# Last feed-forward product with standing weights and 512 moving tokens, in a four-block kernel

## What is computed

```python
h = silu(_tlin(x, w1_w, w1_s)) * _tlin(x, w2_w, w2_s)     # 128 -> 512
h = gelu(_tlin(h, h1_w, h1_s))                            # 512 -> 512, exact gelu
h = gelu(_tlin(h, h2_w, h2_s))                            # 512 -> 512
return _tlin(h, w3_w, w3_s)                               # 512 -> 128, added to x
```

## Time and profile before

| what | value |
|---|---|
| median of 3 runs | 1786.47 us (1783.78 to 1786.57) |
| profiled execution, its own time | 1786.55 us |
| its span, first to last instruction | 1781.5 us |
| stage two, from 1387 us to the end | some 394 us |
| one sequence in the steady part of stage two | 22.67 us |
| busy of the span: PE, DVE, ACT, POOL | 84%, 85%, 72%, 62% |

### The profile page before, as it was taken

The page is one execution under the profiler, slowest core; times in us unless marked ns, Lnnn a source line. Parts: engine busy times, 40 slices in busy tenths (PEclk is TensorE's granted clock), DMA queues, the critical chain, the costliest instruction groups (busy, mean ns, idle before and its releaser), DMA issues. The chain is left out here.

```text
span 1781.5 us, 24641 instructions
## 1 busy us (share of the span) xinstructions
PE 1502.4 (84%) x8039; PEld 807.3 (45%) x8039; DVE 1519.0 (85%) x2837; ACT 1284.4 (72%) x2176; POOL 1103.6 (62%) x987
## 2 busy tenths in 40 slices
PE   4245788888889888888888888888898799999997
PEld 1122343333334333333433334333434588888886
DVE  6899999999999999999999999997331688988883
ACT  5665888988989898898989889895555454444441
POOL 5884776868577686867768586775122255555552
PEclk9996999999999999999999999999999699999998
DMA  4000000000000000000000000000200000000000
GB/s 136 0 1 0 18 13 7 19 1 19 1 19 16 4 19 1 18 1 19 17 3 19 1 19 1 18 15 5 84 3 17 1 7 12 13 13 13 13 13 19
DMA packets 14543, 27.41 MB, mean 15 GB/s; under 512 B 3837, under 2 KB 4550, under 8 KB 13898
## 3 DMA queue, kind: packets, MB, share of 16 engines
q1 hardware_dynamic: 14410, 25.79, 5.2%
HBM read 9.00 MB, written 4.19 MB: 7 GB/s over the span
## 5 line engine op out<-in xcount | busy, mean ns | idle before, releaser
L616 POOL TENSOR_TENSOR sum_fast<-sum_fast,state_fast 128x512 f32<-128x512 f32 x448 | 573.9, 1281 | 78.1 <-DVE state_fast L598 38.0
L598 DVE TENSOR_TENSOR_SCAN state_fast<-state_fast,bank 128x512 f32<-128x512 f32 x512 | 602.7, 1202 | 0.7 <-ACT bank L567 0.7
L1008 ACT ACTIVATE prob_fast<-bank 128x1024 f32<-128x1024 f32 x320 | 326.0, 1020 | 122.1 <-PE bank L992 111.7
L992 PE MATMUL bank<-stacks_fast 64*128 64x512 f32 (+3 forms) x2048 | 361.4, 462 | 50.0 <-ACT prob_fast L1008 46.6
L583 ACT ACTIVATE state_fast<-chan_all_kept,neg_a_fast 128x512 f32<-128x512 f32 x512 | 340.1, 713 | 10.6 <-POOL sum_fast L616 8.5
L1052 POOL TENSOR_SCALAR_AFFINE_SELECT prob_fast<-prob_fast 128x512 f32<-128x512 f32 x256 | 159.9, 636 | 293.6 <-ACT prob_fast L1008 292.1
L992 PEld LDWEIGHTS bank<-stacks_fast 64*128 64x128 f32 x2048 | 170.7, 185 | 250.0 <-ACT prob_fast L1008 150.8
L1069 PE MATMUL bank<-prob_fast,v_ext_fast 128*32 128x512 f32 (+3 forms) x2048 | 177.7, 442 | 8.1 <-POOL prob_fast L1052 7.5
L670 PE MATMUL bank<-resid_m_fast,xnt_g_fast 128*128 128x512 f32 x256 | 137.2, 637 | 34.5 <-DVE gate_fast L751 33.1
L701 PE MATMUL bank<-we_t_fast,xnt_g_fast 128*128 128x512 f32 x256 | 133.7, 633 | 2.5 <-DVE own_fast L822 2.5
L1545 ACT ACTIVATE full_fast<-bank,sh_kept 128x512 f32<-128x512 f32 x64 | 44.1, 689 | 122.4 <-PE bank L1455 122.4
(11 more groups left out here) (204 smaller groups left out, 2596.1 us busy)
## 6 DMA issues: line engine op xcount, KB each, us to landing
stacks_fast<-parts_fast SPq DMA_DIRECT2D x128, 64.0 KB
stacks_fast<-rest_fast SPq DMA_DIRECT2D x128, 32.0 KB
out_x<-f_out_fast SPq DMA_DIRECT2D x16, 256.0 KB, 2.0
x_res_kept<-in_x SPq DMA_DIRECT2D x1, 2048.0 KB, 13.7
chan_all_kept<-in_h_t SPq DMA_DIRECT2D x2, 1024.0 KB, 7.0
x_res_kept<-in_x SPq DMA_DIRECT2D x1, 1024.0 KB, 9.3
chan_all_kept<-in_w_t SPq DMA_DIRECT2D x3, 256.0 KB, 3.9
x_res_kept<-in_x SPq DMA_DIRECT2D x2, 256.0 KB, 3.3
```

What stands on the lines that cost most here:

```text
L598: dve.tensor_tensor_scan(h[:], h[:], self.banks[0][:], 0.0, ALU.mult, ALU.add).then_inc(self.v_scan.sem)
L616: pool.tensor_tensor(total[:], total[:], h[:], ALU.add).then_inc(self.p_sum.sem)
L992: ins = pe.matmul(self.scores(b, step)[:, c:c + SEQ - P * kt], rows[:, 1, h // 2, P * kt:P * kt + P], rows[:, 0, h // 2, P * kt:SEQ], star ...
L1008: act.activation(self.probs[u % 2][:, i * 1024:(i + 1) * 1024], self.scores(b, 5 * g + n)[:], ACT.Exp, scale=SCALE).then_inc(self.a_prob.sem)
```

## The change

The roles in `pe_f_out` are turned round. Now a 128x128 block of w3 stands and 512 tokens move: 4 blocks x 2 parts = 8 matmuls of 512 columns, into the same bank 6. The result has features on the partitions, so ScalarE applies the scale per partition on its way to a new SBUF tile `f_y` (`act_f_out`), and TensorE transposes it back with four transposes into bank 6. VectorE then only adds x. `pe_f_out` becomes two parts with other work between them. The due times of all of stage two are new.

```diff
-PERIOD, F_PERIOD = 78858, 24000
+PERIOD, F_PERIOD = 78858, 24942
...
-    "dve_f_compare": [12000, 36000, 60000, 84000, 108000, 264000],
+    "dve_f_compare": [6614, 44499, 65808, 85662, 133514, 262523],
...
-    "pe_f_turn": [4882],
-    "pe_f_a": [23496, 28976, 34167, 40976],
-    "pe_f_h1": [49477, 55366, 61366, 67234],
-    "pe_f_h2": [82270, 90000, 96000, 102000],
-    "pe_f_out": [114000],
...
+    "pe_f_turn": [211],
+    "pe_f_a": [25282, 28956, 36953, 39884],
+    "pe_f_h1": [51210, 57446, 62584, 67158],
+    "pe_f_h2": [87141, 88084, 92093, 98074],
+    "pe_f_out": [120397, 125914],
+    "act_f_turned": [6894],
+    "act_f_a": [26460, 26589, 28156, 34176, 35350, 40669, 43363, 47697],
+    "act_f_h1": [53878, 60344, 66151, 70704],
+    "act_f_h2": [85441, 90486, 93291, 104297],
+    "dve_f_norm": [-10860, 2411],
+    "dve_f_a": [20033, 23713, 30717, 40552],
+    "dve_f_h1": [50283, 55752, 69033, 69889],
+    "dve_f_h2": [85303, 87183, 97740, 102867],
+    "dve_f_out": [130010],
+    "pool_f_a": [26172, 30002, 36630, 43301],
+    "pool_f_h1": [60478, 71228],
+    "pool_f_h2": [96573, 106621],
...
+    "act_f_out": [122422],
...
-        self.s3_row = sb("s3_row", [P, DM])
+        self.s3 = sb("s3", [P, 1])
...
+        self.f_y = sb("f_y", [P, SEQ])
...
         if b:
-            pe.wait_ge(self.v_f_out.sem, self.v_f_out.at(b - 1, 0))
+            pe.wait_ge(self.v_f_out.sem, self.v_f_out.at(b - 1))
+        for mt in range(MT):
+            for i in range(parts):
+                ins = pe.matmul(banks[6][:], w["w3_t"][:, mt * DM:(mt + 1) * DM], self.f_h2[s][mt][:, i],
+                                start=(mt + i == 0), stop=(mt == MT - 1 and i == parts - 1))
+        ins.then_inc(self.t_f_out.sem)
+        yield
+        pe.wait_ge(self.a_f_out.sem, self.a_f_out.at(b))
         for k in range(NT):
-            for mt in range(MT):
-                for i in range(parts):
-                    ins = pe.matmul(banks[6][:, k * P:(k + 1) * P], self.f_h2[s][mt][:, i, k * P:(k + 1) * P],
-                                    w["w3_t"][:, mt * DM:(mt + 1) * DM], start=(mt + i == 0), stop=(mt == MT - 1 and i == parts - 1))
-        ins.then_inc(self.t_f_out.sem)
+            ins = pe.transpose(banks[6][:, k * P:(k + 1) * P], self.f_y[:, k * P:(k + 1) * P], self.ident[:])
+        ins.then_inc(self.t_f_back.sem)
...
+    def act_f_out(self, b):
+        act = self.act
+        yield
+        act.wait_ge(self.t_f_out.sem, self.t_f_out.at(b))
+        if b == 0:
+            act.wait_ge(self.ld_scale.sem, self.ld_scale.at(0, 4))
+        else:
+            act.wait_ge(self.t_f_back.sem, self.t_f_back.at(b - 1))
+        act.activation(self.f_y[:], self.banks[6][:], ACT.Identity, scale=self.s3[:, 0:1]).then_inc(self.a_f_out.sem)
...
-        dve.wait_ge(self.t_f_out.sem, self.t_f_out.at(b))
+        dve.wait_ge(self.t_f_back.sem, self.t_f_back.at(b))
         if b > 1:
             dve.wait_ge(stored.sem, stored.at(b // 2 - 1))
-        dve.tensor_tensor(out[:], banks[6][:].rearrange("p (k f) -> p k f", k=NT),
-                          self.s3_row[:].unsqueeze(1).to_broadcast([P, NT, DM]), ALU.mult).then_inc(self.v_f_out.sem)
-        dve.wait_ge(self.v_f_out.sem, self.v_f_out.at(b, 0))
-        dve.tensor_tensor(out[:], out[:], self.x(b), ALU.add).then_inc(self.v_f_out.sem)
+        dve.tensor_tensor(out[:], banks[6][:].rearrange("p (k f) -> p k f", k=NT), self.x(b), ALU.add).then_inc(self.v_f_out.sem)
```

More of the change, by code:

```diff
@@ L79 @@
     "pool_masks": [207664, 213107, 214759, 219781, 229386, 230861, 231669, 241828, 246004, 256415, 259423, 262536],
-    "sp_f": [128010],
-    "pe_f_flags": [143063],
-    "dve_f_setup": [0],
-    "dve_f_compare": [12000, 36000, 60000, 84000, 108000, 264000],
-    "dve_f_flags": [31738, 151738],
+    "sp_f": [309895],
+    "pe_f_flags": [131944],
+    "dve_f_setup": [-4007],
+    "dve_f_compare": [6614, 44499, 65808, 85662, 133514, 262523],
+    "dve_f_flags": [118829, 196838],
     "dve_clips": [209645, 216532, 217073, 219208, 231511, 234380, 237882, 242646, 246379, 250401, 256536, 260365],
@@ L201 @@
     "t_f_h2": MT, "a_f_h2": MT, "v_f_h2": MT, "v_f_l2": MT // 2, "p_f_l2": MT // 2,
-    "t_f_out": 1, "v_f_out": 2,
+    "t_f_out": 1, "a_f_out": 1, "t_f_back": 1, "v_f_out": 1,
 }
@@ L373, in sp_weights @@
         sp.dma_start(self.w_raw["w3_t"], t["w3_t"]).then_inc(self.ld_w3_t.sem, 16)
-        for key, dst in (("s1", self.s1), ("s2", self.s2), ("sh1", self.sh1), ("sh2", self.sh2), ("s3_row", self.s3_row)):
+        for key, dst in (("s1", self.s1), ("s2", self.s2), ("sh1", self.sh1), ("sh2", self.sh2), ("s3", self.s3)):
             sp.dma_start(dst[:], t[key]).then_inc(self.ld_scale.sem, 16)
@@ L1647, in sp_f @@
         stored = (self.store0, self.store1)[b % 2]
-        self.sp.wait_ge(self.v_f_out.sem, self.v_f_out.at(b, 1))
+        self.sp.wait_ge(self.v_f_out.sem, self.v_f_out.at(b))
         self.sp.dma_start(self.t["out"][:, b * NT:(b + 1) * NT], self.f_out[b % 2][:]).then_inc(stored.sem, 16)
@@ L1691, in scalar_program_two @@
             strands += [("act_f_turned", b, self.act_f_turned(b)), ("act_f_a", b, self.act_f_a(b, general)),
-                        ("act_f_h1", b, self.act_f_h1(b, general)), ("act_f_h2", b, self.act_f_h2(b, general))]
+                        ("act_f_h1", b, self.act_f_h1(b, general)), ("act_f_h2", b, self.act_f_h2(b, general)),
+                        ("act_f_out", b, self.act_f_out(b))]
         in_order(F_PERIOD, strands)
@@ L1766, in layouts @@
         "sh1": tiles(i["L1_ffn_h1_s"]), "sh2": tiles(i["L1_ffn_h2_s"]),
-        "s3_row": c(np.broadcast_to(i["L1_ffn_w3_s"], (P, DM))),
+        "s3": c(i["L1_ffn_w3_s"].reshape(P, 1)),
     }
```

## The result

| | before | after |
|---|---|---|
| median of 4 runs on one chip | 1785.12 us (1783.61 to 1786.57) | 1761.72 us (1760.25 to 1762.28) |
| ratio | | 0.9868, 95% interval 0.9851 to 0.9885 |
| span of the profiled execution | 1781.5 us | 1758.4 us |

The change takes 23.4 us off. Forecast were 1766.6 us, 19.9 us less, with a range from 1762: the kernel came out 0.3 us under it. Of the 4.9 us between 1766.6 and 1761.72, 3.5 are gain that I had not counted (23.4 - 19.9), and 1.35 is the level of the kernel before in these runs (1785.12 against 1786.47). The change of level alone is larger than the 0.3 us; what has to be explained are the 3.5.

A forecast was written before the change was run, and what follows sets the result against it. TensorE was taken to bound the steady part. The terms -18.9 + 0.7 + 1.0 - 1.0 - 1.7 = -19.9 us gave a span of 1761.6, plus 5.05 outside it, 1766.6 us; range 1762 to 1774.

The forecast's parts named there:

- Steady part: Steady sequences of stage two: TensorE falls from 22.67 to 21.41 us each, -1.26, so -18.9 us over fifteen.
- The place with 0.1 us of slack: Steady part, W2 of a2: VectorE's input done at 6.4 us, PE there at 6.5; the tightest of the new waits.
- rival 1: Steady part: VectorE's lag reaches PE each period, 4 to 10 us in all, say 1773 us; chance 0.14.
- Rival 2: Steady part: PE waits for ScalarE between product and transposes and the kernel gets slower, 1804 us; chance 0.03.
- Rival 3: Last product: a matmul costs only its columns, so nothing is saved and transposes add 4 us, 1790 us; chance 0.01.
- The filling: Pipeline filling after the beginning of stage two: VectorE as loaded as before, 1.6 us of idle PE left unchanged.
- VectorE in the steady part: VectorE per steady sequence: busy time falls from 19.51 to 18.22 us, slack 3.19 us.
- Comparisons: Two large VectorE comparisons, now about 0.8 of a period apart, less well covered by slack: +0.7 us, bounds 0 and 3.
- Beginning: Start of stage two: first a0 2.1 us later behind sequence 1's turn, 0.5 and 0.4 back: +1.0, bounds 0 and 3.
- Idle PE ahead of the product of sequence 14 and elsewhere: Near the end: PE's 0.7 us wait ahead of sequence 14's last product and the pipeline refill go, -1.0 us.
- End: From sequence 15's last h2 to the last addition: 9.4 to 7.7 us, -1.7, bounds -2.8 and -0.9.
- Rival 5: More comes back than counted: tail at its best, no cost at start or comparisons; 1763 us and below; chance 0.07.

The follow-up runs named there:

- e3: The changed kernel with the four transposes issued right behind the last product, so TensorE waits for ScalarE's scaling in each sequence; 1774.64 us.
- e1: The changed kernel's new form of the last product, but in the order (due times) of the kernel before; 1764.12 us, ratio 0.9886 to the kernel before.
- e2: The kernel before, with its old form of the last product, given the new due times; 1784.34 us, ratio 1.0002 to the kernel before.
- e5: The changed kernel itself, unchanged, run again; 1760.42 us, ratio 0.986 to the kernel before.
- e6: The new form in the old order once more, same kernel as e1; 1763.8 us, ratio 0.9884 to the kernel before.
- e11: The kernel before plus unread transposes at the beginning of stage two only, to keep the clock up; 1785.11 us, ratio 1.0002.
- e8: The changed kernel plus unread transposes at both ends of stage two where TensorE only waits, to keep the clock up; 1759.01 us.
- e12: The changed kernel plus two extra unread GpSimd subtractions of 256 columns behind each of GpSimd's a parts; 1771.81 us, ratio 0.9927 to the kernel before.
- e4: The changed kernel, but VectorE first copies bank 6 to SBUF and then adds x, two instructions instead of one; 1765.07 us.
- e7: The changed kernel with the turn of sequence 1 moved back behind a0 of sequence 0; 1759.71 us, ratio 0.9856 to the kernel before.

## Why the prediction missed, point by point

**Steady part: right.** -1.26 per sequence, -18.9 in fifteen; measured 22.67 to 21.41. A further 0.4 came in sequence 14, whose transposes back fall in a gap of PE. The place with 0.1 us of slack (the W2 product of a2) held in every period, so rival 1 did not occur. Rival 2 needed 2.6 us of lateness of ScalarE and there was none; e3 shows the wait if the slack is taken away. Rival 3 fell with 1.87 us for the product.

**The filling: 0 forecast, -2.7 measured. This is the step that failed.** "VectorE is as loaded as before there, so I leave it" put the term at nothing. VectorE's load was not what set the loss: the loss was a clock at half over the first h1 group and four places where PE waits or is slowed, and two of these places go back to ScalarE. Measured by group, 1.4 came back in the first h1 group, which ran at full clock, and 1.3 because two tanh's no longer came late; the waits behind meetings with GpSimd stayed, at +0.3 and -0.2, and these four make the 2.7 to 0.1. The prediction had seen the same cause ahead of the first h1 ("the turned tile's cast no longer stands between two tanh's", 0.5), and had said of the clock only that it may rise later. It rose earlier. e1, e2, e5 and e6 show that all this goes with the order and not with the form; e11 and e8 show 1.0 for the clock itself, all of it in the first h1 group, and 1.5 to 1.7 for the rest. That ScalarE's place for the tanh makes 1.3 of it is read from the rows; no run moves that alone.

**VectorE in the steady part: mis-sized.** "VectorE falls to 19.51 - 1.97 + 0.68 = 18.22" gives the old order's durations to the new order. Measured 15.6 per sequence. I had written in the place on rival 1 that the subtraction takes 1.66 only when GpSimd is at work, and then used 1.66 as if it were its price. It is the price of a meeting, and the order decides how many there are. Shown for the order by e1 and e2, for GpSimd by e12. In the steady part this is worth nothing; it is worth the 0.7 us of the next term.

The Trainium skill (SBUF — State Buffer, "SBUF: two separate sides") says that VectorE and GpSimd share one pair of ports and that an operation of VectorE with two SBUF inputs and one of GpSimd that reads SBUF exclude each other: the one that starts first has the pair for its whole instruction, and the other waits. The traces agree: 0.69 or 1.66 us for the subtraction, 1.52 for GpSimd's when it comes second, and 0.68 for those that read PSUM and SBUF (L1632, L1578).

**Comparisons: +0.7 forecast, 0.0 measured.** The sum had 4.6 us against a slack of 3.2. With VectorE at 15.6 the slack is 5.8, and the two comparisons, though closer together, are covered. In the same order, e4 with VectorE at 17.3 and a slack of 4.1 pays 3.5, and e2 with a slack of 22.67 - 17.8 = 4.9 pays 2.2. e1, with the comparisons a period apart and a slack of 3.4, pays 1.4. The same mis-sized term.

**Beginning: +1.0 forecast, +0.7 measured.** e7 confirms the mechanism: with the turn behind a0, 1.5 to 1.7 us come back (2.1 forecast), and the 12.0 that is left is 1.0 under the kernel before, where 0.5 + 0.4 was forecast.

**Idle PE ahead of the product of sequence 14 and elsewhere: -1.0 forecast, -0.5 measured.**

**End: -1.7 forecast, -1.4 measured** (9.4 to 8.0; the product 2.83, not 2.6). e8 shows that half clock makes 1.1 of the 8.0.

**Sum.** -18.9 - 0.4 + 0.7 - 2.7 + 0.0 - 0.5 - 1.4 = -23.2. Stage one ended 0.9 us earlier in this execution, and what stands behind the last addition took 1.1 more: -23.0, where the spans differ by 23.1. Against the -19.9 of the forecast, the filling is 2.7 of the difference, the comparisons 0.7, the beginning 0.3 and sequence 14's transposes 0.4; idle PE and the end, 0.5 and 0.3 less than forecast, go the other way. Rival 5, more comes back than counted, is what happened. One of its reasons held, the free comparisons; the other two (the end at its best, the start free) did not, and the largest part, the filling, is not among them. The range's low end was built from these reasons and so had no term for it.

**What stays open.** The 1.7 us for the order in the filling is a difference of two single traces, e11 and after. The filling loses 5.2 to 5.8 in the three traces of the old order without added transposes, and 2.7 to 3.4 in the nine of the new order with GpSimd's usual work; the steps within each are mostly the first h1 group, that is, the clock. Which due time brings the clock up earlier, and what the tanh's place alone is worth, was not tried. Whether another order would bring VectorE below 15.6 was not tried; it would buy nothing in the steady part, where PE has no idle time.

## What to carry to other kernels

Where a pipeline fills, ask which wait ends last at each place, on every engine, and what the clock is there, before the term is put at nothing. Here one engine's load was the same and the filling still gave 2.7 us, some half of it where the clock had been low and half where two instructions of ScalarE had come late.

A mean duration in a trace may be a mean of two values, one free and one after a meeting with another engine. Before such a row is used as a price for a new order, look at the single instructions, and give the term both bounds: here it was 2.6 us of VectorE per sequence. What that is worth depends on the place: nothing in the steady part, where PE has no idle time, and some 3 us where one large piece of work falls on VectorE (e4).

## What the runs showed of the hardware that I had not expected

- VectorE's cast, which reads one SBUF tile, took 934 ns on average in e12 and 518 in the filling of the changed kernel. Singly they take 0.42 where nothing is met; in the changed kernel some take 0.92 or 0.93, and a few 1.52 to 1.56, beside a GpSimd subtraction. The four instructions of a normalization, which read one SBUF tile too, take 1.11 with GpSimd idle and 2.11 or 3.08 beside one or two subtractions. So instructions with one SBUF input are held up too.
- Half clock at the last product is not fixed: in e1 the clock stayed full to the end without any help (end 6.9 us), in e6, the same kernel, it did not (8.3). Nor did it fall in e12 (6.9). This moves 1.4 us between runs of one kernel.
- With stage one the same in all, stage two's first normalization began anywhere from 1384.5 to 1389.9 us over 14 profiled executions, and the time outside the span was 1.85 us in the changed kernel's profiled execution, 5.05 in that of before. A single span thus says little below 5 us; the losses by stretch say more.
- A wait of PE costs more than its length: in e3 the four transposes behind a wait took 0.65 us, not 0.44; in the filling of the kernel before, the wait of 0.63 us and the three groups around it lose 1.2.
